# Splitting the hinge sum into two rounded halves on one tile, with two output passes instead of three

## What is computed

```python
s = jnp.einsum('btd,dm->btm', x, Win) + bin_           # 512 -> 64
h = jax.nn.relu(s[..., None] * W1 + b1)                # 16 hinges for each of 64
g = jnp.einsum('btmh,mh->btm', h, W2) + b2             # their weighted sum
out = jnp.einsum('btm,md->btd', g, Wout) + bout        # 64 -> 512
...
x = _layernorm(x + L0_attn(x)); x = _layernorm(x + L0_ffn(x))
```

## Time and profile before

| | |
|---|---|
| median of three runs | 1397.43 us |
| the profiled execution | 1396.98 us, of which the span of instructions is 1395.2 us |
| PE busy | 1298.3 us, 93% |
| ACT busy | 1167.7 us, 84% |
| DVE busy | 1108.5 us, 79% |
| POOL busy | 660.7 us, 47% |

### The profile page before, as it was taken

The page is one execution under the profiler, slowest core; times in us unless marked ns, Lnnn a source line. Parts: engine busy times, 40 slices in busy tenths (PEclk is TensorE's granted clock), DMA queues, the critical chain, the costliest instruction groups (busy, mean ns, idle before and its releaser), DMA issues. The chain is left out here.

```text
span 1395.2 us, 28156 instructions
## 1 busy us (share of the span) xinstructions
PE 1298.3 (93%) x7118; PEld 854.7 (61%) x7118; DVE 1108.5 (79%) x4547; ACT 1167.7 (84%) x2640; POOL 660.7 (47%) x1642
## 2 busy tenths in 40 slices
PE   6981989999999999999999999999999999999974
PEld 5650566666676666666666666666766666554442
DVE  2986887898888888888888888888888888754554
ACT  2660756789999999999999999999999999988883
POOL 1330333345555555555455555555555554545544
PEclk9995999999999999999999999999999999999995
DMA  5380786555565555555555655655655555577743
GB/s 180 90 216 12 175 232 205 182 182 173 191 206 178 200 204 176 204 197 177 209 190 181 212 183 189 212 179 192 207 177 200 195 181 201 186 237 257 249 118 72
DMA packets 91849, 258.33 MB, mean 185 GB/s; under 512 B 15731, under 2 KB 15731, under 8 KB 75286
## 3 DMA queue, kind: packets, MB, share of 16 engines
q1 hardware_dynamic: 91670, 256.39, 56.6%
HBM read 206.00 MB, written 50.33 MB: 184 GB/s over the span
## 5 line engine op out<-in xcount | busy, mean ns | idle before, releaser
L619 PE MATMUL bank<-G_sb,pT 128*128 128x512 f32 x1024 | 460.7, 593 | 0.0
L619 PEld LDWEIGHTS bank<-G_sb,pT 128*128 128x128 f32 x1024 | 184.9, 191 | 183.4 <-issue 183.4
L1041 DVE SCALAR_TENSOR_TENSOR acc<-hinge,w2c,acc 128x512 f32<-128x512 f32 x224 | 167.6, 748 | 107.5 <-ACT hinge L734 107.3
L999 DVE MAX8 top<-bank 128x8 f32<-128x32 f32 x2048 | 212.5, 182 | 38.8 <-issue 38.7
L431 POOL TENSOR_TENSOR shift_sq<-sum,per_row_sq 128x1 f32<-128x1 f32 x256 | 89.3, 349 | 248.7 <-DVE y_sb L893 248.5
L734 ACT ACTIVATE hinge<-s_sb,b1c,w1c 128x512 f32<-128x512 f32 x256 | 206.0, 808 | 0.0
L548 PE MATMUL bank<-A_hi,xT_lo 128*128 128x512 f32 x512 | 203.7, 398 | 0.0
L546 PE MATMUL bank<-A_hi,xT_hi 128*128 128x512 f32 x512 | 203.6, 398 | 0.0
L547 PE MATMUL bank<-A_lo,xT_hi 128*128 128x512 f32 x512 | 203.4, 397 | 0.0
L719 ACT ACTIVATE unread<-y_sb,shift_sq 128x512 bf16<-128x512 f32 x256 | 184.0, 719 | 18.7 <-POOL minus_mean L433 18.7
L893 DVE SCALAR_TENSOR_TENSOR y_sb<-bank,y_sb 128x512 f32<-128x512 f32 x256 | 169.2, 663 | 13.4 <-PE bank L646 13.1
(11 more groups left out here) (119 smaller groups left out, 2536.7 us busy)
## 6 DMA issues: line engine op xcount, KB each, us to landing
G_sb<-G_of_heads SPq DMA_DIRECT2D x128, 1024.0 KB, 5.4
x_sb<-in_L_attn_query_dram SPq DMA_DIRECT2D x128, 256.0 KB, 4.7
y_sb<-in_L_attn_query_dram SPq DMA_DIRECT2D x256, 128.0 KB, 5.4
out_dram<-o_sb SPq DMA_DIRECT2D x256, 128.0 KB, 4.7
G_of_heads<-y_sb SPq DMA_DIRECT2D x64, 256.0 KB, 3.9
y_sb<-in_L_attn_Wk_dram SPq DMA_DIRECT2D x1, 1024.0 KB, 5.6
y_sb<-in_L_attn_Wq_dram SPq DMA_DIRECT2D x1, 1024.0 KB, 8.4
y_sb<-in_L_attn_Wv_dram SPq DMA_DIRECT2D x1, 1024.0 KB
```

Of the source, the lines that this page charges most:

```text
L619: mm = nc.tensor.matmul(o_ps[i % 2][:], pT[:, bass.ds(pair_place(turn, i) + (i % H * C + c) * P, P)], G_sb[:, i % GR, c, :], start=(c == 0 ...
L999: mx = nc.vector.max(top8[:, h, :], z_ps[i % 2][:, h * S:(h + 1) * S])
L1041: nc.vector.scalar_tensor_tensor(acc[:], hinge[:, k % HR, :], w2c[:, k:k + 1], acc[:], ALU.mult, ALU.add).then_inc(s_acc, 1)
```

## The change

The two halves of `acc` are now added before the product. ACT copies the upper half of `acc` onto partitions 0 to 63 of a new tile `both`; POOL adds the lower half to it; ACT writes the rounded sum on partitions 0 to 63 of a new tile `split`; POOL writes the rest on its partitions 64 to 127. One pass with the doubled Wout_hi then multiplies both hi and lo, and a second multiplies by Wout_lo, so that there are two passes beside the bias, where there were three.

Four more edits concern the end of the program. From slot 128 on, the Win product goes to the bank that the transposes of x no longer need (`s_place`); the outputs from number 110 on alternate between two banks (`f_place`); DVE, no longer ACT, normalises y and copies its transpose (`vector_finishes`). The hinges of the last group are made four in a slot, it is split two slots earlier and on DVE, and its split has a tile of its own.

```diff
+        LAST = TILES - GROUP
+        ALONE_S = TILES - LAG_YT
+        ALONE_F = TILES + UNROLL - LAG_OUT
+        def s_place(i):
+            return xT_ps if i >= ALONE_S else ys_ps
+        def f_place(i):
+            return uT_ps if i >= ALONE_F and i % 2 else f_ps
+        def hinges(turn, j, half):
+            n = turn * UNROLL + j - LAG_HINGE
+            lead, q = n - n % GROUP, n % GROUP
+            if 0 <= lead < LAST:
+                return [(lead, 2 * q + half)]
+            if lead == LAST and 2 * q < GROUP:
+                return [(lead, 4 * q + 2 * half), (lead, 4 * q + 2 * half + 1)]
+            return []
+        def split_lead(turn, j):
+            n = turn * UNROLL + j - LAG_SPLIT
+            if n == LAST - 2:
+                return LAST
+            return n if 0 <= n < LAST and n % GROUP == 0 else None
...  GpSimd, behind the two norm calls
-                    pool.wait_ge(s_acchi, group_of(turn, i) + 1)
-                    nc.gpsimd.tensor_tensor(acc_lo[:], acc[:], acc_hi[:].bitcast(F32),
-                                            ALU.subtract).then_inc(s_acclo, 1)
+                    pool.wait_ge(s_upper, lead // GROUP + 1)
+                    nc.gpsimd.tensor_tensor(both[0:M, :], acc[0:M, :], both[0:M, :], ALU.add).then_inc(s_both, 1)
+                    pool.wait_ge(s_hi, lead // GROUP + 1)
+                    nc.gpsimd.tensor_tensor(split[M:P, :], both[0:M, :], split[0:M, :].bitcast(F32),
+                                            ALU.subtract).then_inc(s_lo, 1)
+                    pool.wait_ge(s_lo, lead // GROUP + 1)
...  TensorE
-                    nc.tensor.matmul(f_ps[:], pick_c[:], bout_rows[:], start=True, stop=False)
-                    nc.tensor.matmul(f_ps[:], acc_hi[:, here], Wout_hi[:], start=False, stop=False)
-                    nc.tensor.matmul(f_ps[:], acc_hi[:, here], Wout_lo[:], start=False, stop=False)
-                    nc.tensor.matmul(f_ps[:], acc_lo[:, here], Wout_hi[:], start=False, stop=True).then_inc(s_f, 1)
+                    nc.tensor.matmul(f[:], pick_c[:], bout_rows[:], start=True, stop=False)
+                    nc.tensor.matmul(f[:], parts[:, here], Wout_hi[:], start=False, stop=False)
+                    nc.tensor.matmul(f[:], parts[:, here], Wout_lo[:], start=False, stop=True).then_inc(s_f, 1)
...  ScalarE, behind the copies into s_sb
-                    nc.scalar.copy(acc_hi[:], acc[:]).then_inc(s_acchi, 1)
+                    act.wait_ge(s_acc, (lead // GROUP + 1) * KH)
+                    if lead > 0:
+                        act.wait_ge(s_lo, lead // GROUP)
+                    nc.scalar.copy(both[0:M, :], acc[M:P, :]).then_inc(s_upper, 1)
...  ScalarE, behind the normalised y
-                if in_range(turn, j, LAG_Y):
+                if in_range(turn, j, LAG_Y) and not vector_finishes(turn):
...
+                    act.wait_ge(s_both, lead // GROUP + 1)
+                    if 0 < lead < LAST:
+                        act.wait_ge(s_f, lead)
+                    nc.scalar.copy(split_of(lead)[0:M, :], both[0:M, :]).then_inc(s_hi, 1)
...  VectorE, ahead of the second residual
+                if split_lead(turn, j) == LAST:
+                    dve.wait_ge(s_upper, TILES // GROUP)
+                    nc.vector.tensor_tensor(both[0:M, :], acc[0:M, :], both[0:M, :], ALU.add).then_inc(s_both, 1)
+                    dve.wait_ge(s_hi, TILES // GROUP)
+                    nc.vector.tensor_tensor(last_split[M:P, :], both[0:M, :], last_split[0:M, :].bitcast(F32),
+                                            ALU.subtract).then_inc(s_lo, 1)
+                if in_range(turn, j, LAG_YT) and vector_finishes(turn):
+                    dve.wait_ge(s_yT, base + i + 1)
+                    nc.vector.tensor_copy(yT[:].rearrange("p c n -> p (c n)"), ys_ps[:]).then_inc(s_yTc, 1)
...  VectorE, behind the finished rows
+                if in_range(turn, j, LAG_Y) and vector_finishes(turn):
+                    nc.vector.tensor_scalar(y_sb[:, i % YR, :], y_sb[:, i % YR, :], rstd1[:, i % 2:i % 2 + 1],
+                                            shift1[:, i % 2:i % 2 + 1], ALU.mult, ALU.add).then_inc(s_y, 1)
```

More of the change, by code:

```diff
@@ L138, in build_kernel @@
         acc = sb("acc", [P, GROUP * P])
-        acc_lo = sb("acc_lo", [P, GROUP * P], F32R)
-        acc_hi = sb("acc_hi", [P, GROUP * P], F32R)
+        both = sb("both", [P, GROUP * P])
+        split = sb("split", [P, GROUP * P], F32R)
         sum2 = sb("sum2", [P, 2])
@@ L254, in vector_finishes, with split_of @@
             return isinstance(turn, int) and turn >= TILES // UNROLL
+        LAST = TILES - GROUP
[18 more added lines that the diff above has]
+            return n if 0 <= n < LAST and n % GROUP == 0 else None
+        def split_of(lead):
+            return last_split if lead == LAST else split[:]
         def so_far(turn, j, lag):
@@ L600, in slot @@
                     pe.wait_ge(s_y, base + i + 1)
-                    if not isinstance(turn, int) or base + i >= 1:
-                        pe.wait_ge(s_sc, 4 * (base + i))
+                    if base + i >= 1:
+                        pe.wait_ge(s_yTc, base + i)
+                        if s_place(base + i - 1) is ys_ps:
+                            pe.wait_ge(s_sc, 4 * (base + i))
                     for c in range(C):
@@ L628, in slot @@
                             tokens = slice(t * HALF, (t + 1) * HALF)
-                            mm = nc.tensor.matmul(ys_ps[t * M:(t + 1) * M, 0:HALF], Win_sb[:, c, :],
+                            mm = nc.tensor.matmul(s_ps[t * M:(t + 1) * M, 0:HALF], Win_sb[:, c, :],
                                                   yT[:, c, tokens], start=(c == 0), stop=(c == C - 1))
@@ L723, in make_hinge @@
             def make_hinge(turn, j, half):
-                i = j - LAG_HINGE
-                lead = i - i % GROUP
-                if not in_range(turn, 0, -lead):
-                    return
-                base, g, k = turn * UNROLL, group_of(turn, lead), 2 * (i % GROUP) + half
-                if k == 0:
-                    act.wait_ge(s_sc, 4 * (base + lead + GROUP))
-                if not isinstance(turn, int) or base + lead > 0 or k >= HR:
-                    act.wait_ge(s_acc, g * KH + k - HR + 1)
-                nc.scalar.activation(hinge[:, k % HR, :], s_sb[:, (lead // GROUP) % 2, :], ACT.Relu,
-                                     bias=b1c[:, k:k + 1], scale=w1c[:, k:k + 1]).then_inc(s_hinge, 1)
+                for lead, k in hinges(turn, j, half):
+                    g = lead // GROUP
+                    if k == 0:
+                        act.wait_ge(s_sc, 4 * (lead + GROUP))
+                    if lead > 0 or k >= HR:
+                        act.wait_ge(s_acc, g * KH + k - HR + 1)
+                    nc.scalar.activation(hinge[:, k % HR, :], s_sb[:, g % 2, :], ACT.Relu,
+                                         bias=b1c[:, k:k + 1], scale=w1c[:, k:k + 1]).then_inc(s_hinge, 1)
             def slot(turn, j):
@@ L792, in slot @@
                     nc.scalar.copy(xT_hi[:].rearrange("p c n -> p (c n)"), xT_ps[:]).then_inc(s_xhi, 1)
-                if in_range(turn, j, LAG_YT):
+                if in_range(turn, j, LAG_YT) and not vector_finishes(turn):
                     i = j - LAG_YT
@@ L1025, in hinge_step @@
             def hinge_step(turn, j, half):
-                base = turn * UNROLL
-                i = j - LAG_HINGE
-                first = i - i % GROUP
-                if not in_range(turn, 0, -first):
-                    return
-                g, k = group_of(turn, first), 2 * (i % GROUP) + half
-                dve.wait_ge(s_hinge, g * KH + k + 1)
-                if k == 0:
-                    if not isinstance(base, int) or base + first > 0:
-                        dve.wait_ge(s_acclo, g)
-                    nc.vector.tensor_scalar(acc[:], hinge[:, k % HR, :], w2c[:, k:k + 1], b2c[:],
-                                            ALU.mult, ALU.add).then_inc(s_acc, 1)
-                else:
-                    dve.wait_ge(s_acc, g * KH + k)
-                    nc.vector.scalar_tensor_tensor(acc[:], hinge[:, k % HR, :], w2c[:, k:k + 1],
-                                                   acc[:], ALU.mult, ALU.add).then_inc(s_acc, 1)
+                for lead, k in hinges(turn, j, half):
+                    g = lead // GROUP
+                    dve.wait_ge(s_hinge, g * KH + k + 1)
+                    if k == 0:
+                        if lead > 0:
+                            dve.wait_ge(s_both, g)
+                        nc.vector.tensor_scalar(acc[:], hinge[:, k % HR, :], w2c[:, k:k + 1], b2c[:],
+                                                ALU.mult, ALU.add).then_inc(s_acc, 1)
+                    else:
+                        dve.wait_ge(s_acc, g * KH + k)
+                        nc.vector.scalar_tensor_tensor(acc[:], hinge[:, k % HR, :], w2c[:, k:k + 1],
```

(1 more changed line is left out.)

40 lines of the change are left out of this document (28 added, 12 removed).

## The result

The changed kernel takes 1377.05 us, the median of four runs (1376.4 to 1377.42); the kernel before took 1397.72 in the four runs beside them. The ratio is 0.9854, with a 95% interval of 0.9837 to 0.9871. The forecast was 1360.7 with a range of 1351 to 1372: the sign was right, and the time lies 5 us outside the range. The profiled execution took 1377.39 us, span 1375.6, 17.1 us more than the 1360.3 worked out for it.

The account below looks back on a forecast made before the run. PE's stream of matmuls was taken to bound the loop; gains of 21.7 (loop), 13.8 (thin loop) and 1.2 (drain) sum to 36.7 us, from 1396.98 to 1360.3, with 0.45 for the median 1360.7; range 1351 to 1372.

Parts of the forecast that it names:

- The loop: Outputs 0 to 93, bound by PE: one pass less saves 0.233 us in each of 93 steps, 21.7 us.
- A: Rival: ACT becomes the bound in the loop, half of the pass's gain (10.9 us) is lost, 1371.6 us; chance 0.12.
- E: Rival: the removed pass was partly covered, so the loop loses 10.9 us of its gain, 1371.6 us; chance 0.03.
- D: Rival: ACT waits for POOL's addition in each split slot; with 3 us late, 16.6 us slower, 1414; chance 0.03.
- with the knock-on on y 1.0 us for a group: Thin loop: late hinges delay DVE's copy of yT 0.7 us; with y 1.0 per group, 0.25 per step.
- The floor: Thin loop: PE's own work with one pass less and no waits for Win product copies, 5.42 us a step.
- the chain's 4.0 us: Thin loop split slot: copy, addition, copy, subtraction take 4.0 us before the means, making squares and hinges late.
- The gain of 0.60: Thin loop: a step falls from 6.28 on the mean to 5.67 us, 13.8 us over 23 steps.
- 2.0 us more on the path: Drain: split of outputs 120 to 123, two copies and two POOL instructions instead of one each, costs 2.0 us.
- a gain of 2.8: Drain: ACT's period over three slots falls from 5.03 to about 4.1 us without y and yT, gaining 2.8.
- Rival B: Thin loop gains only the pass, 5.4 us, since DVE holds back the Win product path; 1369.1 us; chance 0.10.
- the prediction's own sign of being wrong: Among the signs: thin loop steps above 6 us, with PE waiting for DVE's L993.

Follow-up runs that it names:

- e5: Changed kernel with the old split and three passes, keeping the edits to the end, but the last group split like the others: 1384.94 us, ratio 0.9917.
- e4: Changed kernel, but the last group has two hinges in a slot and is split in its own slot on POOL like the others: 1378.68 us.
- e6: Changed kernel, but VectorE does the split's addition and subtraction for the groups from tile 96 on: 1365.19 us, ratio 0.9777.
- e1: Kernel before plus only the new split and two passes, without the four edits to the end: 1396.21 us, ratio 0.999.
- e2: Changed kernel, but ACT keeps the normalised y and the copy of its transpose to the end: 1378.3 us, ratio 0.986.
- e7: Changed kernel, but VectorE's two instructions of the last split stand behind the second norm's sum and the last output's scaling: 1375.02 us.
- e11: Changed kernel with e6 and e7 together: 1362.94 us, ratio 0.9762.
- e8: Changed kernel, but from tile 104 on all four instructions of a split stand one behind another on VectorE: 1370.56 us, ratio 0.9814.
- e12: e11, but y and its transposes' copy move to VectorE from output 102 on in place of 94: 1363.9 us, ratio 0.9765.

## Why the prediction was wrong

**The loop: right.** 21.7 us forecast, 21.9 measured, with a group at 867.64 / 23.25 = 37.32 us (37.33 forecast). The pass was worth 0.23 us, and not the 131 ns of the Trainium skill's "TensorE: Matmul & The Clock Gate", "Back-to-back issue gap"; rivals A and E fall, and D in the loop. The prices taken for the unknown instructions held: ACT's 64x512 copy 0.62 us, POOL's 64x512 1.26 to 1.29, where 0.62 and 1.30 were taken.

**The thin loop: the step that failed** is "with the knock-on on y 1.0 us for a group". The floor was right (5.42 forecast, 5.38 measured), the chain's 4.0 us too, and the lateness of the squares. But the cover was checked in one place: "PE needs the rest at L643 [...] 3 us later" is true in the loop, where PE has the x transposes and the scores between. In a thin slot PE reaches its output product 1.4 us before the chain's end, and that wait was not in the sum at all; only the copy of yT was. A group costs (71.68 - 12 x 5.38) / 3 = 2.4 us over the floor, not 1.0. That makes 71.68 us from output 104 to 116, where 75.29 - 12 x 0.60 = 68.1 were forecast: 3.6 us of the error.

**The first eleven steps** are the larger part. The gain of 0.60 was worked out from two steady slots and then used for all 23, though the mean of the stretch was 6.65 and not 6.28; that difference is the first eleven steps, 77.58 / 11 = 7.05 us, which carry the last sparsemax work and of which the prediction has no row. Forecast 77.58 - 6.6 = 71.0, measured 81.07: 10.1 us of the error. e5 shows that the edits to the end alone save 3.1 there; e4 against e5, that the new split costs 6.4; 3.0 of the whole stand in the trace as matmuls at the low clock behind waits. The split acts indirectly here: PE waits 10.3 us for yT and for the sparsemax, in e5 3.9, in e6 6.6, and never for the split. Which of the late instructions on ACT and DVE makes `pT` and `differs` late was not followed further.

**The drain:** "2.0 us more on the path" for the split; it was 5.5 (e1 against before) and 5.6 (e4 against e5), so that a forecast gain of 1.2 became a loss of 3.0, outside the bounds of -2 and +5. The other large term, "a gain of 2.8" for taking y and yT off ACT, is not there either: e2 leaves both on ACT, and its drain takes 56.9 us, the changed kernel's 57.2. Put together from the runs, the drain is 54.2 us, less 0.8 for the edits to the end (e5), 5.6 more for the split (e4), less 1.8 for the early split of the last group. In e7 2.0 of it came back by order alone. The rest, between e11's drain of 54.8 and e5's 53.45, stays open.

These make 3.6 + 10.1 + 4.2 = 17.9, less 0.2 in the loop and 0.6 in the fill, which is chance: the 17.1 us. That e6 reaches the thin loop nearly as forecast (141.1 us against 139.1) with nothing changed but the engine of two instructions, and with it their place in the order, is what shows the cause: POOL's part in the split. Whether it costs more by its own 1.26 us twice or by the means behind it was not told apart. Rival B named DVE's delay of yT and 5.4 us of gain. The delay was there, as the prediction's own sign of being wrong had it: PE waits 4.6 us for L993 in the thin loop (2.13, 0.86 and three times 0.54), as much as for POOL's subtraction (1.43, 1.70 and 1.43), and the gain was 0.1. But more than half of it isn't DVE's own load, since in e6, where DVE has the split too, only the first of these waits is left (2.12). Rival D's mechanism, ACT waiting for the addition, was real, but in the thin loop, where the prediction had not worked it out: L839 waited 8.9 us in six splits there.

## What to carry to other kernels

A chain that is hidden in a program's full loop must be checked once more in every stretch with fewer stages, since the work that hid it is just what is missing there: ask for each result when its reader comes by, per stretch. A stretch whose mean step differs from the two slots one has read is to be read elsewhere too before a gain is multiplied by its length. And an engine that is best placed in the loop can be the wrong one at the end: moving two instructions from GpSimd to VectorE for the seven groups ahead of the last, and putting those of the last behind the norm's sum, gave 14 us.

## What the runs showed of the hardware

On GpSimd an instruction with two operands on 64 partitions costs as much as on 128: 1.26 us (L508, L510) against 1.30 in the earlier trace rows. On ScalarE too, 0.62 against 0.62. VectorE does the same 64x512 in 0.68 to 0.69, about half of GpSimd's time. Halving the partitions saves nothing on any of these two, so "half of a tile" was in effect a second whole instruction.

The clock fell behind single waits of PE of 2.45, 2.75 and 2.99 us, with the engine busy before: granted 0.83, 0.83 and 0.70 over these steps. In L659 (L663 in e1) alone that cost 1.2 to 2.3 us on top of each wait. But the length of the wait does not settle it. In e1 PE waits 2.99 us in three steps, and they take 8.55, 10.01 and 11.26 us at granted clocks of 1.00, 0.83 and 0.70, so the clock costs nothing, 1.5 or 2.7 us. e8 is the same program as the changed kernel up to output 103: there the clock fell at output 95, behind a wait of 2.12 us (granted 0.92), and stayed at 1.00 at output 101, behind 2.46, while in the changed kernel it stayed at 1.00 behind 2.13 and fell behind 2.45. In e6 a wait of 2.33 us at output 98 left it at 1.00, in e12 it fell behind 2.11 (0.81). So one or two us between two profiles in this stretch can be the clock alone.
